# Expert stages written out expert by expert, with waits on constants, in place of loops over pairs of experts

## What is computed

```
x = x + 0.5 * ffn(layernorm(x))          # 16 experts, each takes its best 512 tokens, hidden 1024, gated by silu
x = x + attn_and_moe(layernorm(x))       # linear attention; then 8 experts, top 2 of each token, hidden 1024, gelu
x = x + 0.5 * ffn(layernorm(x))
# one feed-forward expert, xin = its 512 tokens:
#   eo = (silu(xin @ gw.T + gb) * (xin @ up_w.T + up_b)) @ down_w.T + down_b, scaled by the token's score, added to the tokens
# one MoE expert, xf[tok] = its up to 1280 tokens:
#   h  = gelu(xf[tok] @ W1 + b1) @ W2 + b2, scaled by the token's gate, added to the tokens
```

## Time and profile before

| | |
|---|---|
| median of 3 runs | 2702.67 us |
| the profiled execution, its own time | 2704.92 us |
| its span, first to last instruction | 2702.8 us |
| mean granted TensorE clock | 0.907 |
| PE busy | 2322.4 us, 86% |
| DVE / POOL / ACT busy | 66% / 33% / 31% |
| PE in the three expert stages, busy of stretch | 553.72 of 553.80, 490.87 of 544.30, 553.72 of 553.80 us |
| DMA over the span | 227.45 MB, mean 84 GB/s |

### The profile page before, as it was taken

How to read it: one execution, slowest core, us unless ns; L and a number is a source line. 1 busy time by engine, 2 the same in 40 slices (tenths; PEclk the granted TensorE clock), 3 DMA queues, 4 the chain that set the end, 5 groups by cost and what they waited for, 6 DMA issues and landing times. The chain is left out here.

```text
span 2702.8 us, 42010 instructions
## 1 busy us (share of the span) xinstructions
PE 2322.4 (86%) x13308; PEld 1996.8 (74%) x13308; DVE 1772.5 (66%) x3693; ACT 848.1 (31%) x1542; POOL 901.4 (33%) x965
## 2 busy tenths in 40 slices
PE   5897999999994888863898888992789799999997
PEld 4676888888883666551788888892578688888886
DVE  3674777777773999753555555552477477777775
ACT  4221333333331333310233333332322233333332
POOL 2210233333323777511134344423320133333332
PEclk7997999999996888955889999996799799999999
DMA  4001444444432000031243344325100344444442
GB/s 155 20 24 65 131 126 129 124 129 124 129 95 56 24 31 29 30 94 43 62 74 74 69 74 74 73 28 141 38 24 32 112 130 124 128 125 128 124 124 51
DMA packets 154422, 227.45 MB, mean 84 GB/s; under 512 B 33344, under 2 KB 105024, under 8 KB 154176
## 3 DMA queue, kind: packets, MB, share of 16 engines
q1 hardware_dynamic: 103472, 157.95, 19.1%
q0 software_dynamic: 39936, 55.93, 11.8%
q10 hardware_dynamic: 10896, 12.07, 1.3%
HBM read 171.49 MB, written 54.39 MB: 84 GB/s over the span
## 5 line engine op out<-in xcount | busy, mean ns | idle before, releaser
L998 ACT ACTIVATE me_act_f<-me_in,me_bias 128x512 f32<-128x512 f32 (+1 forms) x192 | 119.1, 620 | 316.8 <-PE me_in L109 299.8
L107 PE MATMUL f1e_in<-f1e_xt_hi,f1e_w_hi 128*128 128x512 f32 x512 | 203.2, 397 | 2.1 <-DVE f1e_xt_lo L1058 2.0
L107 PE MATMUL f2e_in<-f2e_xt_hi,f2e_w_hi 128*128 128x512 f32 x512 | 203.1, 397 | 2.1 <-DVE f2e_xt_lo L1058 2.0
L109 PE MATMUL f1e_in<-f1e_xt_hi,f1e_w_lo 128*128 128x512 f32 x512 | 202.4, 395 | 0.0
L109 PE MATMUL f2e_in<-f2e_xt_hi,f2e_w_lo 128*128 128x512 f32 x512 | 202.2, 395 | 0.0
L108 PE MATMUL f1e_in<-f1e_xt_lo,f1e_w_hi 128*128 128x512 f32 x512 | 201.8, 394 | 0.0
L108 PE MATMUL f2e_in<-f2e_xt_lo,f2e_w_hi 128*128 128x512 f32 x512 | 201.8, 394 | 0.0
L998 ACT ACTIVATE f1e_silu<-f1e_in,f1e_bias 128x512 f32<-128x512 f32 x128 | 88.1, 689 | 341.9 <-PE f1e_in L109 273.7
L998 ACT ACTIVATE f2e_silu<-f2e_in,f2e_bias 128x512 f32<-128x512 f32 x128 | 88.1, 689 | 341.0 <-PE f2e_in L109 291.7
L1087 DVE CAST me_act_hi<-me_act_f 128x512 fp32r<-128x512 f32 (+1 forms) x192 | 73.9, 385 | 179.4 <-ACT me_act_f L998 169.2
L107 PE MATMUL me_down<-me_w_hi,me_act_hi 128*128 128x256 f32 x640 | 186.4, 291 | 0.0
(11 more groups left out here) (427 smaller groups left out, 7097.8 us busy)
## 6 DMA issues: line engine op xcount, KB each, us to landing
f1e_raw<-in_ffn_w SPq DMA_DIRECT2D x128, 384.0 KB
f2e_raw<-in_ffn_w SPq DMA_DIRECT2D x128, 384.0 KB
me_raw<-in_moe_w SPq DMA_DIRECT2D x64, 256.0 KB
f1s_x_all<-in_x SPq DMA_DIRECT2D x8, 512.0 KB, 9.7
f_h<-f1s_h ACTq DMA_DIRECT2D x8, 512.0 KB, 3.1
after_ffn<-f1s_out SPq DMA_DIRECT2D x8, 512.0 KB, 3.0
ma_x_all<-after_ffn SPq DMA_DIRECT2D x32, 128.0 KB
after_moe<-ma_x_all SPq DMA_DIRECT2D x32, 128.0 KB, 1.7
```

The costliest lines, as they stand in the source:

```text
L107: pe.matmul(out, lh, rh, start=first, stop=False, skip_group_check=True)
L109: return pe.matmul(out, ll, rh, start=False, stop=last, skip_group_check=True)
L998: act.activation(dst[:, st % 2, 0:n], ps_in[st % 2][0][:, 0:n], func, bias=bias[:, b, f:f + 1]).then_inc(silu_done, 1)
```

## The change

`experts` calls `one` for every expert with Python numbers. The five engines' programs are otherwise the same, and in the same order. `left` is 2 for all but the last two experts, as before.

```diff
-        def experts(eng, one):
-            with eng.Fori(0, E // 2 - 1) as i:
-                one(i * 2, 0, 2)
-                one(i * 2 + 1, 1, 2)
-            one(E - 2, 0, 1)
-            one(E - 1, 1, 0)
+        def experts(one):
+            for e in range(E):
+                one(e, e % 2, min(2, E - 1 - e))
...
-            experts(sp, one)
+            experts(one)
```

More of the change, by code:

```diff
@@ L915, in one @@
                 pool.nop().then_inc(landed, 1)
-            experts(pool, one)
+            experts(one)
         @block.tensor
@@ L977, in one @@
                     down(e, S - LAG + st)
-            experts(pe, one)
+            experts(one)
         @block.scalar
@@ L1038, in one @@
                         next_slice(e + 1, st, left - 1)
-            experts(act, one)
+            experts(one)
         @block.vector
@@ L1135, in one @@
                         add_bias(e, S - LAG + st, b)
-            experts(dve, one)
+            experts(one)
 def ffn(nc, tag, x_in, acc, gate_w, shared_w, ffn_w, ffn_b, ffn_db, consts):
```

## The result

The changed kernel took 2656.36 us in the median of three runs (2654.03 to 2657.89), the kernel before 2702.67. The ratio is 0.9839, with a 95% interval of 0.9821 to 0.9858. The prediction was 2701.3 us with a range of 2682 to 2718; the time came within 4 us of rival 1 in its whole form (2660 us, chance 0.08).

The account below looks back on a forecast made before the run. PE bounds it: always busy in feed-forward, waiting in MoE mostly for activations beside gathers. Terms 0 - 0.44 - 0.92 = -1.4 us from 2704.92 give 2703.5; the median lies 2.25 lower: 2701.3 us, range 2682 to 2718.

Parts of the forecast that it names:

- rival 1: MoE expert changes: PE's waits there come from the loop; whole 2660 us, chance 0.08; in part 2688 us, chance 0.23.
- Feed-forward at 0: Feed-forward experts: PE fully busy, 34.57 us looped or written out, so writing out 28 experts changes 0.
- Rival 2: Feed-forward stages: code fetched during gathers holds PE up, about 20 us slower, 2723 us; chance 0.24.
- over 100 were expected: Sign on the instruction packet queue q8: its packets grow from 66 to over 100.
- Branch -0.44 us: MoE stage, second long branch: without it PE's 1.93 us "issue" wait ends 0.44 us sooner.
- entry -0.92 us: Way into the MoE loop: PE's 0.92 us of "issue" goes with the entry's instructions.
- the bound of 0: MoE loop entry: gain is 0 if the instructions' supply, not the loop, causes the "issue" time.
- The rule of the Trainium skill: MoE stage's two long branches: taken branches stall for a fetch; by this rule alone the gain is 8.2 us.
- the term for wait values that become constants: All expert stages: constant waits and addresses, without register instructions, lie under PE's matmuls and give 0.
- The part that was left to the loop, 14 us: MoE expert changes: if all six lose about 2.4 us of waits, the gain is 14, giving 2688 us.
- The price of rival 1: MoE expert changes: 30 us from shorter waits and 12 from PE's clock, giving 2660 us.
- Its sign: MoE stage: waits for `me_act_lo` falling from 44 to about 14 us would show rival 1 right.

Follow-up runs that it names:

- g3: Kernel before, loops kept, with only one of ten row tiles gathered per MoE expert, the other nine left as zeros: 2640.2 us.
- h1: Changed kernel with only one of ten row tiles gathered per MoE expert, the other nine left as zeros: 2637.6 us.
- h2: Kernel before, loops kept and everything computed, with each MoE expert's ten gathers issued in five pairs two steps apart: 2649.7 us.
- h3: Changed kernel, everything computed, with each MoE expert's ten gathers issued in five pairs two steps apart: 2643.9 us.
- e2: Changed kernel with ScalarE (ACT) alone back in the loop over pairs of experts: 2687.8 us.
- e4: Changed kernel with SP and POOL together back in the loop over pairs of experts: 2685.4 us.
- g1: Kernel before with only the MoE stage written out, both feed-forward stages still looped over pairs: 2674.7 us.
- the control: Changed kernel run again unaltered, on another chip beside the kernel before: 2664.6 us, ratio 0.9846.
- m1: Changed kernel, still written out, with every MoE-stage wait compared with a register plus a constant, the register set per expert: 2700.22 us.

## Why the prediction was wrong, step by step

**Feed-forward at 0: right.** 34.57 us again, and the last feed-forward's stage from first to last matmul takes 558.7 us before and 559.3 after.

**Rival 2, slower by collisions of fetches with gathers: dead.** The packets came (99 on q8, over 100 were expected), one each 23 us where 20 were estimated, and cost TensorE nothing in either feed-forward stage.

**Branch -0.44 us and entry -0.92 us: neither is in its rows.** The entry's "issue" stands at 0.90 us in written-out code too, so the loop's entry isn't its cause and the bound of 0 holds. The 1.93 us of "issue" that the branch was given stand at the change from expert 3 to 4 in written-out code as well (1546.65), one step later. What the loops cost in the MoE stage where bursts don't hide it is 0.9 us by g3 against h1 and 0.5 by h2 against h3, single runs each: the size was near, the reading wasn't.

The rule of the Trainium skill ("Runtime: NRT & Kernel Launch", instruction fetch mechanics), a stall at each jump back to code that is not at hand, would give 8.2 us. The two long branches, 3.6 and 4.6 us, are there, but these runs show at most 0.9 us of them in the stage's time.

**The step that failed** is in rival 1: "the gather is the likelier cause, and it stays". The gather is the cause, and g3 shows it. But it was weighed against the loop as if only one could be. The wait is what a burst of gathers costs a program that does register work ahead of its waits, and taking away either factor takes most of it away: of 48.7 us of TensorE's idle time at the gathers the changed kernel has 15.7, and h2, in its whole stretch, 14.0 where 53.4 stood. So the term for wait values that become constants was put at 0, and the gathers were taken as a cause that the change leaves alone, where the two together made 49 us. The part that was left to the loop, 14 us, was priced by another difference (1.49 and "issue" against 0.19). A chance of 0.08 was too small for a case that one row (5.35 us, below) was left to exclude.

Two readings led there. The first: the wait of 5.35 us at 1716.40 was held against rival 1 because TensorE was then "already in written-out code". That looked at one engine. The loop's own line in the kernel before, all engines, around that wait:

```profile
...
L859 PEldq COMPARE_BRANCH  x1: 83/83/83, 1705.6 to 1705.6; - x1
...
L859 ACTq COMPARE_BRANCH  x1: 40/40/40, 1714.0 to 1714.0; - x1
...
L859 DVEq COMPARE_BRANCH  x1: 55/55/55, 1715.8 to 1715.8; - x1
...
L859 POOLq COMPARE_BRANCH  x1: 40/40/40, 1738.8 to 1738.8; - x1
...
```

ScalarE left its loop at 1714.0 and VectorE at 1715.8, just as that wait ended; POOL, which issued the gathers, 22 us later. The wait was made while three engines were in looped code, and e2 to e4 show that one alone brings back about half of the idle time (35.3 to 37.5 us, between 22.1 and 48.7). The second: the 4.28 us at 1307.63 were counted for the gather because expert 0 has them too, but they stand in the loop's first pass. The changed kernel has 1.36 and 0.53 us in their place.

**The price of rival 1 was near.** It took 30 us for the waits and 12 for the clock; 33.2 and 15.9 were measured. Its sign came too: the waits for `me_act_lo`, which were to fall from 44 to about 14 us, fell to 7.3, with 9.8 more that now end as "issue".

**The sizes of the sum hid this.** The feed-forward stages hold a looped and a written-out expert of equal length, and that was carried over to the MoE stage by its steady part (42.00 of 42.00 us). But a stage that waits has no such sample: the only written-out change of experts there had no gather beside it.

**What is still open.** How register operations lengthen the waits isn't shown, nor that they do it by letting fewer updates through. It can't be only the time that such operations take on TensorE or ScalarE, since looping SP and POOL does as much as looping VectorE. Whether the updates are held back by POOL's issuing of the gathers or by their traffic wasn't separated. Nor is it shown why g1 lies 10 us above the control, which part of m1 does it (the operation at the wait, the wait's own form, the register set or the branch per expert), or why attention became 2.8 us shorter.

## What to carry over

A wait that stands only beside X isn't proved to be X's alone: ask for a sample without the change under test and with X, and if there is none, give the product of both a real chance. Before a row is read as "in code of the new form", look at where every engine of the chain is, not only the one that waits. And a long burst of indirect gathers is worth breaking up first: in pairs two steps apart it cost next to nothing, which was worth more here (59 us with the loops kept) than what made the burst cheaper (46 us).

## What the runs showed of the hardware

- While POOL issues ten indirect gathers in a row (12.5 to 13.7 us), semaphore updates of TensorE come up to 7.3 us late. With pairs of gathers 3 to 5 of 82 come over 1.3 us late, at most 3.5, and the MoE stage is as long as without the burst (497.0 and 496.5 us in h2 and h3, 496.8 and 495.9 in g3 and h1); four in a row (5.3 us, the feed-forward experts) cost TensorE no idle time either.
- With a register operation ahead of each wait the seven bursts cost TensorE 43.3 to 48.7 us, with constants 15.7 to 25.0.
- 430 us of looped code, 12 experts and more, brought one instruction packet on q14 and none on q8; the same stretch written out brought 19 on q8, at no cost to TensorE.
- A wait of 1.39 us left TensorE's granted clock at 1.00, the upper of its two levels; behind waits of 5.3 and 6.3 us it stood at 0.50.
